# Mamba scan on one core: part of the inflow as a product on TensorE, more of the outflow on GpSimd

## The reference, cut to what matters

```python
delta = softplus(x_act @ dt_proj_w.T + dt_proj_b)      # T x 256
B_p, C_p = split(x_act @ x_proj_w.T)                   # T x 16 each
A = -exp(A_log)                                        # 256 x 16
def step(h, inp):                                      # over the 2048 tokens
    dA = exp(d_i[..., None] * A)
    h = dA * h + (d_i * u_i)[..., None] * B_i[:, None, :]
    y = einsum('bdn,bn->bd', h, C_i)
```

## Time and profile before

| what | value |
|---|---|
| time, median of 3 runs | 1102.28 us (1101.16 to 1107.06) |
| the profiled execution: its own time / its span | 1102.07 us / 1100.1 us |
| scan stage (DVE's first scan to its last but one product with C) | about 767 to 982 us of the span |
| busy in 767 to 982 | DVE 210.43, POOL 209.30, PE 161.41, ACT 108.30 of 215 us |
| mean granted TensorE clock, whole span / that stage | 0.93 / 0.86 |

### The profile page before, as it was taken

The page is one execution under the profiler, slowest core; times in us unless marked ns, Lnnn a source line. Parts: engine busy times, 40 slices in busy tenths (PEclk is TensorE's granted clock), DMA queues, the critical chain, the costliest instruction groups (busy, mean ns, idle before and its releaser), DMA issues.

```text
span 1100.1 us, 11087 instructions
## 1 busy us (share of the span) xinstructions
PE 932.5 (85%) x2909; PEld 547.9 (50%) x2909; DVE 822.2 (75%) x1163; ACT 602.8 (55%) x1095; POOL 679.1 (62%) x469
## 2 busy tenths in 40 slices
PE   6869976688889957899999999987577787887997
PEld 3324432233337725688888888732223333335775
DVE  4895437999965568666666666587999999986755
ACT  5756675300356754455565555686444545545556
POOL 3030134699852133577777777619999999962773
PEclk9989998699999968899999999998788988897999
DMA  2000120000020004377666667302334334424251
GB/s 82 1 0 1 50 77 18 0 0 1 0 71 1 11 19 101 94 157 152 138 151 153 148 141 156 90 0 76 106 108 113 113 103 114 106 72 105 70 145 39
DMA packets 33449, 84.68 MB, mean 77 GB/s; under 512 B 4352, under 2 KB 14208, under 8 KB 29216
## 3 DMA queue, kind: packets, MB, share of 16 engines
q1 hardware_dynamic: 33408, 84.20, 30.5%
HBM read 82.22 MB, written 1.97 MB: 77 GB/s over the span
## 4 chain that ended last, share of the span: by engine, by line
PE 36%; DVE 16%; ACT 3%; issue 3%; POOL 1%; DVEq 0%; ACTq 0%; POOLq 0%
PE ps L630 35%; DVE y L3167 5%; DVE g L3167 5%; DVE tmp L2468 1%; DVE g L2468 1%; DVE rstd L2468 1%; ACT rstd L1440 1%; DVE ps L2468 1%; POOL g L2424 1%; ACT g L1440 1%; ACT ps L1440 1%; DVE normed L2468 0%; ACT sq L1440 0%; ACT parts L1440 0%; DVE g L3123 0%
## 5 line engine op out<-in xcount | busy, mean ns | idle before, releaser
L630 PE MATMUL ps<-parts 128*128 128x512 f32 x1704 | 416.5, 403 | 17.5 <-DVE g L2468 6.2
L630 PEld LDWEIGHTS ps<-parts 128*128 128x128 f32 x1704 | 321.6, 190 | 107.1 <-issue 18.3
L630 PE MATMUL ps<-g,arena 128*128 128x512 f32 (+2 forms) x408 | 191.2, 608 | 26.6 <-POOL g L2351 15.1
L1440 ACT ACTIVATE g<-ps 128x512 f32<-128x512 f32 (+1 forms) x216 | 127.3, 596 | 147.5 <-PE ps L630 143.1
L2302 POOL TENSOR_TENSOR parts<-g,parts 128x512 fp32r<-128x512 f32 x112 | 144.4, 1290 | 60.8 <-ACT parts L1440 57.9
L2468 DVE TENSOR_TENSOR ps<-g,ps 128x512 f32<-128x512 f32 x160 | 111.3, 695 | 94.5 <-PE ps L630 72.8
L1440 ACT ACTIVATE ps<-g,small 128x512 f32<-128x512 f32 x131 | 89.8, 688 | 98.3 <-DVE y L3167 52.9
L630 PEld LDWEIGHTS ps<-g,arena 128*128 128x128 f32 (+1 forms) x408 | 76.9, 197 | 133.1 <-issue 88.9
L1440 ACT ACTIVATE parts<-g 128x512 fp32r<-128x512 f32 (+3 forms) x243 | 125.9, 547 | 24.7 <-DVE g L2468 17.6
L2424 POOL TENSOR_TENSOR g<-g,arena 128x1024 f32<-128x1024 f32 x48 | 113.7, 2396 | 0.1
L2468 DVE TENSOR_TENSOR g<-ps,g 128x512 f32<-128x512 f32 (+1 forms) x140 | 98.9, 706 | 18.1 <-DVE ps L2468 3.3
(11 more groups left out here) (226 smaller groups left out, 1182.2 us busy)
## 6 DMA issues: line engine op xcount, KB each, us to landing
g<-coef_scratch SPq DMA_DIRECT2D x56, 512.0 KB, 6.2
arena<-bc_scratch SPq DMA_DIRECT2D x48, 256.0 KB, 3.3
g<-in_moe_dram SPq DMA_DIRECT2D x34, 192.0 KB, 4.7
g<-coef_scratch SPq DMA_DIRECT2D x24, 256.0 KB, 5.5
sq<-bc_scratch SPq DMA_DIRECT2D x24, 256.0 KB, 3.3
arena<-coef_scratch SPq DMA_DIRECT2D x24, 256.0 KB, 4.3
g<-bc_scratch SPq DMA_DIRECT2D x16, 256.0 KB, 3.3
g<-in_rope_dram SPq DMA_DIRECT2D x1, 2048.0 KB, 8.7
```

The costliest lines, as they stand in the source:

```text
L630: return nc.tensor.matmul(o, lhsT, rhs, start=start, stop=stop, **kw)
L1440: return nc.scalar.activation(o, i, func, **kw)
```

## The change

Three steps of each chunk (n = 6, 10, 14; `BY_PE`, 12 steps in all) get their inflow from PE. For a tile of 128 tokens, the transposed delta u (tokens on the partitions, channels along the free dimension) is the stationary matrix, and a diagonal matrix with B_n of the 128 tokens is the moving one; the product is delta u times B_n with the channels on the partitions. Per step that is eight products 128x128x128 in float32, written into the PSUM banks that held the decays; the decays of these steps go into the SBUF inflow buffer of the step instead, so that the scan again reads one operand from PSUM and one from SBUF. POOL makes no product with B in these steps and SP loads no row.

What this needs: B with the tokens on the partitions (`b_turned` on PE, 16 products with 16 moving columns, and a copy by ACT), delta u turned (`du_into`, eight transposes a chunk on PE, two copies of 128x512 by ACT), and for each of the 12 steps a diagonal matrix (`diag_of_b`, four activations of 128x128 on ACT).

`BY_POOL` becomes all odd steps but the last: 31 steps instead of 24, so DVE makes 33 products with C instead of 40.

The spread B rows stay in the same four slots to the end; slots and semaphore counts go by the number of the row that is used, not by the step. Some semaphores are merged to make room. The diff, cut to its core:

```diff
-BY_POOL = [s for s in range(STEPS) if s % 16 in (1, 3, 6, 8, 11, 13)]
+BY_POOL = [s for s in range(STEPS - 1) if s % 2 == 1]
+BY_PE = [s for s in range(STEPS) if s % 16 in (6, 10, 14)]
+B_ROWS = [s for s in range(STEPS) if s not in BY_PE]
...
         def decays(step, i):
-            return ps[:, DA_BANKS[(2 * step + i) % 3], :]
+            return inflow(step)[:, i, :] if step in BY_PE else flow_bank(step, i)
+        def flow(step, i):
+            return flow_bank(step, i) if step in BY_PE else inflow(step)[:, i, :]
...
# SP
-                        if step >= 4:
-                            sp.wait_ge(s["db_ready"], step - 3)
-                        sp.dma_start(b_copy(step), ...).then_inc(s[f"row_loaded{k}"], 16)
-                        if step - 7 in BY_POOL[:-2]:
-                            load_c(by_pool(step - 7) + 1)
+                        if step not in BY_PE:
+                            use = of_rows(step) - 1
+                            if use >= 4:
+                                sp.wait_ge(s["db_ready"], use - 3)
+                            sp.dma_start(b_copy(use), ...).then_inc(s[f"row_loaded{use % 4}"], 16)
+                        if step - 6 in BY_POOL[:-2]:
+                            load_c(by_pool(step - 6) + 1)
...
# PE
+            def b_turned():
+                for c in range(CHUNKS):
+                    for a in range(TILES):
+                        at = 256 + (c * TILES + a) * 16
+                        last = mm(ps[:, 0, at:at + 16], bc_whole[:, c * N + a * P:c * N + (a + 1) * P], ident[0:96, 0:16])
+                last.then_inc(s["dut_bank"], 1)
+            def du_into(bank, c, half):
+                for a in (2 * half, 2 * half + 1):
+                    for i in range(2):
+                        last = nc.tensor.transpose(ps[:, bank, at:at + P], g[:, 6 + i, ...], ident)
+                last.then_inc(s["dut_bank"], 1)
+            def inflow_by_pe(step):
+                c = step // 16
+                pe.wait_ge(s["x_parts"], diag_parts(step))
+                for i in range(2):
+                    pe.wait_ge(s["hs_done"], 2 * step + i - 2)
+                    for a in range(TILES):
+                        last = mm(flow(step, i)[:, a * P:(a + 1) * P], du_turned(c, a, i),
+                                  b_diag(step)[:, a * P:(a + 1) * P])
+                    last.then_inc(s["x_bank"], 1)
...
             spread_c(0)
+            b_turned()
+            pe.wait_ge(s["du_ready"], 1)
+            du_into(4, 0, 0)
+            du_into(7, 0, 1)
...
                 c, n = step // 16 - 1, step % 16
+                if step + 1 in BY_PE:
+                    inflow_by_pe(step + 1)
                 if step - 3 in BY_POOL:
                     sum_n(step - 3)
...
+                if c < 2 and n in (11, 15):
+                    du_turn(c + 2, n // 15)
                 if step + 1 < STEPS and step + 1 not in BY_POOL:
                     spread_c(step + 1)
...
# ACT
                 for i in range(2):
-                    if 2 * step + i >= 3:
+                    if step in BY_PE:
+                        act.wait_ge(s["hs_done"], 2 * step - 6)
+                    elif 2 * step + i >= 3:
                         act.wait_ge(s["hs_done"], 2 * step + i - 2)
...
+            def diag_of_b(step):
+                act.wait_ge(s["x_parts"], 1)
+                if by_pe(step) > 2:
+                    act.wait_ge(s["x_bank"], 2 * (by_pe(step) - 2))
+                for a in range(TILES):
+                    at = (step // 16 * TILES + a) * 16 + step % 16
+                    last = f(b_diag(step)[:, a * P:(a + 1) * P], ident, ACT.Copy, scale=b_by_token[:, at:at + 1])
+                last.then_inc(s["x_parts"], 1)
...
                 state_step(step)
                 if step == 1:
+                    act.wait_ge(s["dut_bank"], 1)
+                    f(b_by_token, ps[:, 0, 256:512], ACT.Copy).then_inc(s["x_parts"], 1)
+                    du_copied(0, 0)
+                    du_copied(0, 1)
                     act.wait_ge(s["setup_bank"], SETUP["mo_bank"])
                     f(wout_centred, ps[:, 0, 0:256], ACT.Copy).then_inc(s["setup_read"], 1)
                 if step >= 2:
                     save_carry(step - 2)
+                if step + 3 in BY_PE:
+                    diag_of_b(step + 3)
+                if n == 13 and c < 2:
+                    du_copied(c + 2, 0)
+                if n == 1 and 0 <= c < 3:
+                    du_copied(c + 1, 1)
...
# POOL
-                        if step + 4 < STEPS:
+                        if step + 4 in B_ROWS:
                             b_times_du(step + 4)
...
# DVE
                 for i in range(2):
                     dve.wait_ge(s["da_ready"], 2 * step + i + 1)
-                    ins = v.tensor_tensor_scan(states(step % 4)[:, i, :], decays(step, i), inflow(step)[:, i, :],
+                    if step in BY_PE:
+                        dve.wait_ge(s["x_bank"], 2 * by_pe(step) + i - 1)
+                    ins = v.tensor_tensor_scan(states(step % 4)[:, i, :], decays(step, i), flow(step, i),
```

More of the change, by code:

```diff
@@ L430, in decays, with b_copy, du_turned, b_diag @@
         def decays(step, i):
-            return ps[:, DA_BANKS[(2 * step + i) % 3], :]
+            return inflow(step)[:, i, :] if step in BY_PE else flow_bank(step, i)
+        def flow(step, i):
+            return flow_bank(step, i) if step in BY_PE else inflow(step)[:, i, :]
         def two_halves(home, k):
             return home[:, 2 * k * N:2 * (k + 1) * N].rearrange("p (i n) -> p i n", i=2)
-        def b_copy(step):
-            home = arena[0][:, 1792:3840] if step < 48 else g[:, 8, :]
-            return home[:, step % 4 * N:(step % 4 + 1) * N]
+        def b_copy(use):
+            return arena[0][:, 1792 + use % 4 * N:1792 + (use % 4 + 1) * N]
+        def du_turned(c, a, i):
+            at = c % 2 * 1024 + a * 2 * P + i * P
+            return g[:, 8, at:at + P]
+        def b_diag(step):
+            use = BY_PE.index(step) % 2
+            return arena[1][:, 3072 + use * N:3072 + (use + 1) * N]
+        b_by_token = arena[1][:, 128:384]
+        def flow_bank(step, i):
+            return ps[:, DA_BANKS[(2 * step + i) % 3], :]
         def inflow(step):
@@ L458, in by_dve, with by_pe, of_rows, turned_parts @@
             return step + 1 - by_pool(step)
+        def by_pe(step):
+            return sum(k <= step for k in BY_PE)
+        def of_rows(step):
+            return step + 1 - by_pe(step)
+        def turned_parts(c, part):
+            return 1 + part if c == 0 else 3 + 5 * (c - 1) + 3 + part
+        def diag_parts(step):
+            return 3 + 5 * (step // 16) + BY_PE.index(step) % 3 + 1
         block = ctx.enter_context(nc.Block())
@@ L547, in _ @@
                             if use < 4:
-                                sp.wait_ge(s[f"row_loaded{use}"], ROWS_BEFORE[use] + 256)
+                                sp.wait_ge(s[f"row_loaded{use}"], ROWS_BEFORE[use] + B_LOADED)
                             else:
@@ L1266, in row, with du_turn @@
                 return sel_bc[:, n, :]
+            def b_turned():
[7 more added lines that the diff above has]
+                    for i in range(2):
+                        at = (a % 2 * 2 + i) * P
+                        last = nc.tensor.transpose(ps[:, bank, at:at + P], g[:, 6 + i, c * N + a * P:c * N + (a + 1) * P],
+                                                   ident)
+                last.then_inc(s["dut_bank"], 1)
+            def du_turn(c, half):
+                pe.wait_ge(s["du_ready"], c + 1)
+                if c >= 2:
+                    pe.wait_ge(s["x_ready"], x_at(7) + c - 1)
+                if half:
+                    pe.wait_ge(s["x_parts"], turned_parts(c, 1))
+                du_into(4, c, half)
+            def inflow_by_pe(step):
[7 more added lines that the diff above has]
+                    last.then_inc(s["x_bank"], 1)
             def spread_c(step):
@@ L2025, in state_step, with du_copied @@
                       scale=neg_a[:, n + 16 * i:n + 16 * i + 1]).then_inc(s["da_ready"], 1)
+            def du_copied(c, half):
+                act.wait_ge(s["dut_bank"], 2 * c + half + 2)
+                at = c % 2 * 1024 + half * N
+                f(g[:, 8, at:at + N], ps[:, 7 if (c, half) == (0, 1) else 4, :], ACT.Copy).then_inc(s["x_parts"], 1)
+            def diag_of_b(step):
[6 more added lines that the diff above has]
+                last.then_inc(s["x_parts"], 1)
             def save_carry(step):
@@ L2420, in b_times_du @@
                             pool.wait_ge(s["dl_ready"], 2 * CHUNKS)
-                        pool.wait_ge(s[f"row_loaded{step % 4}"], ROWS_BEFORE[step % 4] + 16 * (step // 4 + 1))
+                        use = of_rows(step) - 1
+                        pool.wait_ge(s[f"row_loaded{use % 4}"], ROWS_BEFORE[use % 4] + 16 * (use // 4 + 1))
                         if step >= 4:
@@ L2424, in b_times_du @@
```

(5 more changed lines are left out.)

37 lines of the change are left out of this document (18 added, 19 removed).

## The result

The changed kernel takes 1112.7 us (median of 4 runs, 1111.7 to 1113.3), the kernel before 1103.3 us in the same comparison: a ratio of 1.0071, 95% interval 1.0054 to 1.0088. It is slower, by a little more than what a measurement can tell from no change. The profiled execution took 1113.33 us with a span of 1111.5 us.

The account below looks back on a forecast made before the run. The prediction took DVE as the chain bounding the scan stage, with POOL beside it. From 1102.07 us, -7.8 (DVE) + 3.0 (start) + 8.8 (turns) + 1.0 (other inflows) = +5.0 gave 1107.0 us, range 1097 to 1115.

Parts of the forecast that it names:

- likeliest case: Whole kernel, with turns and start as costed: 1107.0 us, own range 1103.5 to 1110.5, chance 0.50.
- rival 4: POOL runs out in the three full pairs of steps, 1 us in each of four chunks: 1111.0 us, chance 0.08.
- rival 2: PE stays at half clock: start 5.8, nine other inflows 5.4, turns 9.5 us; 1115.0 us, chance 0.18.
- What DVE saves: Scan stage: seven products with C leave DVE at 1.12 us each, 7.8 us less.
- The turns: Scans 22, 38 and 54: DVE waits for PE's inflow queued behind sums, 2.55 us once and 3.15 twice, 8.8 us.
- Rival 3: Weights are not loaded under the products of PE's 128-column inflow: 2.4 us more at the turns, 1109.4 us, chance 0.07.
- The start: Before scan 2: ACT waits for PE's turned B and delta u, so DVE scans about 3.0 us later.
- the prediction's other case: At the start, PE's clock stays low throughout: 40 records take 8.8 us, and the start costs 5.8 us.
- The other nine: Inflows at n = 10 and 14 and in chunk 0: late only at half clock, 1.0 us, bounds 0 and 5.4.
- SP's loads of C: hidden: SP's queue in the scan stage: loads of C stay four products ahead of use and cost nothing.
- Rivals 1 and 4: The first: turns cost nothing, 1097.3 us, chance 0.17; the other: POOL runs out in three full pairs, 1111.0, chance 0.08.
- Nothing gives it back: At the turns, the 8.8 us are not recovered: DVE is the chain, and POOL only runs ahead while it waits.

Follow-up runs that it names:

- spread first and n = 6 early: Changed kernel with the turn's inflow, layer 7's weights, variance product, spread of C and every n = 6 inflow issued earlier, start copies later: 1095.7 us, ratio 0.9921.
- the second profile: The changed kernel measured once more without an edit, against the kernel before: 1113.6 us, ratio 1.0080.
- the three edits: Changed kernel with inflow of steps 22, 38, 54 issued earlier, ACT's start copies moved to step 3, layer 7's weights loaded before the last C row: 1104.9 us, ratio 1.0008.
- the copies later: Changed kernel with ACT's three copies of the start moved from step 1 to step 3: 1111.9 us, ratio 1.0068 to the kernel before.

## Why the prediction was right and where it was not

The measured time lies in the range of 1097 to 1115, which is wide, and above the likeliest case's own range (to 1110.5). The sum gave +5.0 us; the medians give +9.4 and the stage +9.9. I gave no change and slower nearly the same chance (0.42 and 0.41); it is slower by 0.7%. By its number rival 4 (1111.0) lies nearest, but none of its waits for POOL is there. By its mechanism rival 2 (1115.0) does: PE at half clock where it counts, 3.20 us at the second turn where it has 3.15, a start of 5.0 for its 5.8. Yet the sign it named, a granted clock under 0.86 in the stage, is absent (0.88): the mean over the stage does not show the places that count.

- *What DVE saves*, -7.8: confirmed, by the term of the balance and by the run with spread first and n = 6 early (stage -7.5).
- *The turns*, +8.8: measured 9.6, by the mechanism named, and removed by moving one call (`inflow_by_pe`). Nearly all of the 0.8 us more is the second turn, which now begins at half clock. The first half's price, 1.05 us, was right: 16 records take 1.95 us, 0.11 us apart. "TensorE: Matmul & The Clock Gate" of the Trainium skill says in its section "The mechanism" that a weight load overlaps matmuls in flight only when it goes to other rows of the array. This trace disagrees, also for products that are no transposes: in the 1.78 us from 906.16 the products are busy throughout and the loads beside them 1.77 us. Rival 3 falls.
- *The start*, +3.0: mis-sized, measured 5.0. The step that failed is "1.2 GHz for the first two to four us of the burst", taken from a turn with 512-column products. Here PE worked on 16-column products and transposes and stayed at half clock for all 10 us; the prediction's other case (40 records in 8.8 us) had their length right, 8.6 us. Why the clock did not rise stays open.
- *The other nine*, +1.0: mis-sized, measured 3.0, all in chunk 0. The step that failed is that PE is free one sum after DVE's product: the sum of s - 5 is queued behind the same spread, so two sums start then, at half clock after 4 us of rest. The working has a slip besides: 3.4 + 2.0 + 2.0 is 7.4, not 7.6, so each is 0.4 us late and not 0.6. That makes this bound 3.6 instead of 5.4 and rival 2 1113.2.
- *"SP's loads of C: hidden"*: wrong. The rows of C were in time; what stood behind the last of them in the queue, the next layer's weights, was not (+1.5).
- *DVE's waits before the change*: read as 2.9 us in two; there was a third of 0.57 us, at 889.38. Rival 2 says that PE idles 4 to 5 us before each burst; it was 4.61, 2.45 and 2.55 us.
- *The chances*: rivals 2 to 4 and a third of the likeliest case add to 0.50 for slower, of which 0.41 was given.
- *Not foreseen*: the -1.7 us of DVE's three products of delta u. It is the place where POOL stands at their start, so it is largely luck: in the second profile it was -0.8, with the three edits +0.3. Without it the balance lies 6.5 us above the forecast (turns 0.8, start 2.0, the other nine 2.0, weights 1.5, other waits 0.2); with it, 4.8 us. So this term of luck hid part of the error.
- *Rivals 1 and 4*: DVE never waited for POOL in the two profiles of the changed kernel. In the run with the old `BY_POOL`, POOL has 12 products less than before and the time is longer, so POOL's saving gives nothing by itself.
- *"Nothing gives it back"* was right, and there was more: a repaired wait shows the next. Of the 9.6 us, 4.0 came out of the stage at first; from the same queue of PE came the root (1.70 us a turn) and the spread.

## What to carry to other kernels

Work that is moved to an engine with free time costs what stands ahead of it in that engine's queue at the moment it is needed. Add up that queue at the bursts, record by record, against what the waiting engine has left to do. Put what the chain waits for ahead of sums that nobody awaits yet, but only where it is ready: an early instruction that must itself wait holds up all behind it. When a load is delayed, look at what is queued behind it on the same issuing engine.

## What the runs showed of the hardware

The clock. From 768.67 to 778.70 PE was busy 10.02 of 10.03 us, with records of 16 and 128 columns after a rest of 6.7 us, and the granted clock was 0.50 (1.2 GHz) all the while. In the second turn PE rested 3.77 us; its first 512-column sum ran at granted clock 0.50 (3.78 us), and the next four records took 2.17 us, at 0.85 by the mean of the stretch from 900.49 to 902.50.

DVE and POOL. A 128x1024 product of DVE with both operands in SBUF took 1.2 us where POOL was idle at its start and up to 3.3 us where it was not: 1.08 us plus the rest of POOL's product (39 such products in 13 profiles). The products with one operand in PSUM took 1.19 to 1.23 us, also with POOL busy 222.7 of 223 us.

The spread of times. The kernel before took 1101.3 to 1107.8 us in 23 runs of one comparison, and in the profiles the first scan starts between 767.8 and 771.8 us, after layers that no edit touched. The stage in a profile leaves that part out, but it is one execution: the two profiles of the changed kernel give 226.8 and 227.3 us, and with the copies later the profiled execution was 4.5 us under its median.
